# GpSimd's down-weight sums of a batch go behind its output tiles' scale operations, their halves and their store one batch later

## The reference

```
q, k, v = n(x) @ Wq, n(x) @ Wk, n(x) @ Wv            # n: layernorm over the 512 values
scores  = swap(q) @ swap(k).T / 4                     # 512 x 512 per batch: features attend to features
x       = x + n(swap(softmax(scores) @ swap(v)) @ Wo)
gate_w, up_w, down_w = spline(gate_cp), spline(up_cp), spline(down_cp)   # cubic, from few control points
x       = x + n((silu(n(x) @ gate_w.T) * (n(x) @ up_w.T)) @ down_w.T)    # inner width 2048
```

## Time and profile before

| | us |
|---|---|
| median of 3 runs (lowest to highest) | 900.88 (900.14 to 902.31) |
| the profiled execution | 904.34 |
| its span, first to last instruction | 902.5 |
| mean granted TensorE clock | 0.934 |

### The profile page before, as it was taken

How to read it: one execution, slowest core, us unless ns; L and a number is a source line. 1 busy time by engine, 2 the same in 40 slices (tenths; PEclk the granted TensorE clock), 3 DMA queues, 4 the chain that set the end, 5 groups by cost and what they waited for, 6 DMA issues and landing times. The chain is left out here.

```text
span 902.5 us, 19204 instructions
## 1 busy us (share of the span) xinstructions
PE 769.6 (85%) x7152; PEld 513.1 (57%) x7152; DVE 538.8 (60%) x1025; ACT 368.2 (41%) x632; POOL 440.3 (49%) x616
## 2 busy tenths in 40 slices
PE   5686999999999998984666988979879888897986
PEld 3564668776877685762232654636435555563455
DVE  6562753685377545654556667676667676863453
ACT  3321333232323232323445545555445555554541
POOL 4399459545944692032343444434444443543442
PEclk9797799999999998997796999999989999898999
DMA  8246147314741664058224063251622534315122
GB/s 304 105 156 193 66 152 266 122 46 163 245 131 35 196 214 99 2 189 285 84 87 148 6 202 123 91 191 49 198 85 86 188 103 154 128 59 200 48 72 72
DMA packets 64313, 120.54 MB, mean 134 GB/s; under 512 B 12144, under 2 KB 28656, under 8 KB 62192
## 3 DMA queue, kind: packets, MB, share of 16 engines
q1 hardware_dynamic: 64240, 119.53, 40.6%
HBM read 82.94 MB, written 36.57 MB: 132 GB/s over the span
## 5 line engine op out<-in xcount | busy, mean ns | idle before, releaser
L1194 POOL TENSOR_TENSOR act<-inter,act 128x512 f16<-128x512 f32 x128 | 152.5, 1194 | 87.6 <-ACT act L1234 87.4
L1304 DVE SCALAR_TENSOR_TENSOR inter<-ubank,c_up,gated 128x512 f32<-128x512 f32 x128 | 96.0, 750 | 99.3 <-ACT gated L1238 81.9
L1238 ACT ACTIVATE gated<-gbank,c_gate 128x512 f32<-128x512 f32 x128 | 88.0, 687 | 59.2 <-PE gbank L1401 58.9
L1441 PE MATMUL ybank<-down,act 128*128 128x160 f16 x512 | 110.7, 236 | 0.0
L1442 PE MATMUL ybank<-down,act 128*128 128x160 f16 x512 | 109.8, 235 | 0.0
L1443 PE MATMUL ybank<-down,act 128*128 128x160 f16 x512 | 109.7, 235 | 0.0
L1234 ACT CAST act<-inter 128x512 f16<-128x512 f32 x128 | 78.7, 615 | 43.8 <-DVE inter L1304 43.5
L1401 PE MATMUL gbank<-z,s_twice 128*32 128x512 f16 x512 | 53.7, 409 | 44.8 <-DMA z<-token_features 22.9
L897 POOL TENSOR_TENSOR hr<-hmv,heps 128x1 f32<-128x1 f32 x32 | 6.1, 192 | 162.4 <-DVE hmv L926 162.4
L1441 PEld LDWEIGHTS ybank<-down,act 128*128 128x128 f16 x512 | 50.4, 98 | 37.1 <-issue 36.6
L1401 PE MATMUL ubank<-z,s_twice 128*32 128x512 f16 x512 | 53.2, 406 | 19.9 <-DVE inter L1304 19.7
(11 more groups left out here) (190 smaller groups left out, 2178.0 us busy)
## 6 DMA issues: line engine op xcount, KB each, us to landing
x_ln<-x SPq DMA_DIRECT2D x64, 256.0 KB, 3.7
z<-token_features SPq DMA_DIRECT2D x16, 1024.0 KB, 6.6
job<-job_in SPq DMA_DIRECT2D x24, 640.0 KB, 5.4
shared<-x SPq DMA_DIRECT2D x32, 256.0 KB, 2.7
x<-shared SPq DMA_DIRECT2D x32, 256.0 KB, 2.0
token_features<-z_hi SPq DMA_DIRECT2D x64, 128.0 KB
token_features<-z_lo SPq DMA_DIRECT2D x64, 128.0 KB
x_res<-x SPq DMA_DIRECT2D x32, 256.0 KB, 2.7
```

The lines of the kernel that those rows point to most:

```text
L1194: pool.tensor_tensor(hidden[par][:, i, TOK:2 * TOK], inter[:, i % INTERS, :], hidden[par][:, i, 0:TOK], ALU.subtract).then_inc(inter_ready, 1)
L1238: act.activation(gated[:, slot % 2, :], gbank[:], ACT.Silu, scale=c_gate[:]).then_inc(silu_done, 1)
L1304: dve.scalar_tensor_tensor(out=inter[:, i % INTERS, :], in0=ubank[:], scalar=c_up[:], in1=gated[:, i % 2, :], op0=ALU.mult, op1=ALU.mult). ...
L1441: pe.matmul(out, hidden[par][:, r, high], box[:, 0], start=False, stop=False)
```

## The change

GpSimd, in batches 0 to 2: both unit weights first, then the next batch's `ln_scale` and the `y_scale`, then all six sums. In the last batch: unit weights, sums 0 and 1, unit weights, sums 2 to 5, and then the scales, as the sums have no batch behind them. In batches 1 to 3, ScalarE and VectorE take the halves of the batch before in the stages of the Gram matrix and of the first product; the last batch's own stay between its output tiles. SyncE stores a batch's halves behind `store_units` of the next, and issues job loads at the end of the body. The body of batch 0 is written out.

```diff
 SyncE
+            def store_jobs(b):
+                sp.wait_ge(job_ready, held(sp, (b + 2) * JOBS))
+                sp.dma_start(d_dram[held(sp, b)], job_out[:]).then_inc(d_stored, 16)
-            def body(b, more):
+            def body(b, first, more):
...
-                load_job(b, 2)
-                load_job(b, 3)
                 store_units(2 * b, True)
-                load_job(b, 4)
-                load_job(b, 5)
+                if not first:
+                    store_jobs(b - 1)
+                if not more:
+                    load_job(b, 2)
+                    load_job(b, 3)
                 store_units(2 * b + 1, more)
-                if more:
-                    load_job(b + 1, 0)
-                    load_job(b + 1, 1)
+                if not more:
+                    load_job(b, 4)
+                    load_job(b, 5)
...
                 if more:
                     load_res(b + 1, XR - 1)
-                sp.wait_ge(job_ready, held(sp, (b + 2) * JOBS))
-                sp.dma_start(d_dram[held(sp, b)], job_out[:]).then_inc(d_stored, 16)
+                    for k in range(2, JOBS):
+                        load_job(b, k)
+                    load_job(b + 1, 0)
+                    load_job(b + 1, 1)
+                else:
+                    store_jobs(b)
 GpSimd
             def body(b, more):
-                for c in range(2):
-                    sum_job(b, 2 * c)
-                    sum_job(b, 2 * c + 1)
-                    unit_weights(2 * b + c)
-                sum_job(b, 4)
-                sum_job(b, 5)
+                unit_weights(2 * b)
+                if not more:
+                    sum_job(b, 0)
+                    sum_job(b, 1)
+                unit_weights(2 * b + 1)
+                if not more:
+                    for k in range(2, JOBS):
+                        sum_job(b, k)
...
                     y_scale(b, t)
...
+                if more:
+                    for k in range(JOBS):
+                        sum_job(b, k)
 ScalarE (VectorE has the same with evac_lo, mirror_lo, job_lo)
-            def body(b, more):
+            def body(b, first, more):
                 for m in range(K):
                     evac_hi(b, 0, m, ga_hi, m * P, G_SCALE)
                     if m:
                         mirror_hi(b, m - 1)
+                        if not first:
+                            job_hi(b - 1, m - 1)
                 for m in range(K):
                     evac_hi(b, 1, m, tu_hi, 0, 1.0)
...
+                    if not first and m < K - 1:
+                        job_hi(b - 1, K - 1 + m)
...
-                    if 1 <= t <= JOBS:
+                    if not more and 1 <= t <= JOBS:
                         job_hi(b, t - 1)
 each of the four engines
-            with act.Fori(0, B - 1) as b:
-                body(b, True)
-            body(B - 1, False)
+            body(0, True, True)
+            with act.Fori(0, B - 2) as before:
+                body(before + 1, False, True)
+            body(B - 1, False, False)
```

More of the change, by code:

```diff
@@ L309, in _ @@
                 load_res(0, t)
-            with sp.Fori(0, B - 1) as b:
-                body(b, True)
-            body(B - 1, False)
+            body(0, True, True)
+            with sp.Fori(0, B - 2) as before:
+                body(before + 1, False, True)
+            body(B - 1, False, False)
             for q in range(XR):
@@ L567, in body @@
                         mirror_lo(b, m - 1)
+                        if not first:
+                            job_lo(b - 1, m - 1)
                 for m in range(K):
@@ L572, in body @@
                     dve.tensor_copy(xT_lo[:, m, :], tbank[:, 1, :].bitcast(F16)).then_inc(tb_lo, 1)
+                    if not first and m < K - 1:
+                        job_lo(b - 1, K - 1 + m)
                 if more:
@@ L632, in body @@
                                                  op0=ALU.subtract, op1=ALU.add).then_inc(x1_ready, 1)
-                    if 2 <= t < 2 + JOBS:
+                    if not more and 2 <= t < 2 + JOBS:
                         job_lo(b, t - 2)
@@ L683, in _ @@
             scales()
-            with dve.Fori(0, B - 1) as b:
-                body(b, True)
-            body(B - 1, False)
+            body(0, True, True)
+            with dve.Fori(0, B - 2) as before:
+                body(before + 1, False, True)
+            body(B - 1, False, False)
         @block.tensor
```

## The result

| | before | after |
|---|---|---|
| median (lowest to highest), us | 901.48 (900.14 to 902.31), 4 runs | 919.23 (917.79 to 926.13), 4 runs |
| profiled execution / its span, us | 904.34 / 902.5 | 926.13 / 924.3 |
| first matmul of batch 0's output tiles | 105.77 | 91.68 |
| first matmul of the FFN half | 421.37 | 439.91 |

The ratio of after to before is 1.0211, 95% interval 1.0164 to 1.0258. The forecast was 920.1 us, range 907 to 929. A ratio here compares the means of the fast runs, those at most 1.5% above the fastest of their kernel (for after with a fifth, of 919.39 us), while medians and ranges are of all runs, with one slow run each in the first and the third experiment (914.14 and 920.49 us).

What follows compares the result with a forecast made beforehand. The attention half is set by TensorE where GpSimd is early and by GpSimd where late; the FFN half is unchanged. Terms: -13.3 + 2 x 4.5 + 23.5 = +19.2 on median 900.88 gives 920.1 us, range 907 to 929.

Steps and rivals of the forecast that it cites:

- Batch 0: First batch: VectorE's 14.43 us wait for GpSimd's reciprocal deviation goes, fourth product falls from 24.16 to 10.88 us, -13.3 us.
- the bound at -20: Batch 0's largest gain, -20 us, if its third product gets batch 1's pace too.
- The load queue: Sums' loads behind the output tiles, no longer hidden: with 4.1 us loads, six sums take 22.4 us from S.
- S: Start of GpSimd's sums behind a batch's output tiles, from which the prediction counts its GpSimd times.
- Batches 1 and 2: Middle batches: reciprocal deviation 0.7 us late and second unit weights over the softmax normalisation; +4.5 us each, ends 0 and 6.7.
- Batch 3: Last batch: own six sums plus the previous batch's precede the first FFN scale, S + 59.8 for S + 36.3, +23.5 us.
- The halves: ScalarE's and VectorE's halves, moved into the next batch's first two products: taken at nothing; uncovered, each costs 0.8 us.
- (a): Rival: load gap covers the softmax, batch 0 gains 20.0 us, batches 1 and 2 gain 1.2 each; 896.9 us, faster; chance 0.05.
- (b): Rival: last batch's order is felt, middle batches free, batch 0 gains more; 901 to 908 us; chance 0.09 together with (e).
- (c): Rival: slow loads, each 640 KB one 5.1 us or more, and the lock in full; 930 us and up; chance 0.05.
- (d): Rival: batch 0's unit weights end after about 78, VectorE still stalls; 9 us gain left, +23; counted within forecast's 0.81.
- (e): Rival: halves were on the output tiles' path, 14.4 us back, 905.7 us; chance 0.09 together with (b).

Runs made afterwards that it cites:

- The first experiment: Changed kernel, but in the last batch GpSimd takes both unit weights, then the first FFN tiles' scales, its own six sums among and behind them: 905.3 us.
- the third experiment: Changed kernel with the second unit weights of batches 1 and 2 one column wide, their work left out: 914.7 us, ratio to before 1.0091.
- The thin sums: Kernel before the change with batch 0's six sums one column wide, loads and order kept: 893.29 us, ratio to before 0.9878.
- the fourth experiment: Changed kernel with all 48 half operations of ScalarE and VectorE one column wide: 919.52 us, ratio to before 1.0141.
- the last two experiments: Changed kernel with sums 0 and 1 between the unit weights, last batch's scales among its sums: 892.08 us; then also sums 2 and 3 between output-tile scales: 885.01 us.
- the last experiment: Kernel with sums 0 and 1 in the load gap, plus sums 2 and 3 of batches 0 to 2 cut between output-tile scales: 885.01 us, ratio to before 0.9808.

## Why the prediction was right

*Batch 0.* The forecast was that GpSimd's list ends at 72.5, VectorE is free at 73.6, and TensorE is next. Measured: 73.0, 73.1, and 10.88 us for the fourth product, the -13.3 us forecast. The further 6.7 us of the third product, the bound at -20, did not come, since the second unit weights still lie on that softmax. The thin sums show that those 6 us exist.

*The load queue.* S + 22.4 was forecast for the end of the sums, and 140.53 - 118.13 = 22.4 us was measured. Its parts hold too: load 2 was expected at S + 8.9 and sum 2 begins at S + 9.0; load 4 at 16.2 and sum 4 begins at 16.0; load 5 at 19.3 and sum 5 begins at 19.3. The load time chosen (4.1 us, against the median of 5.1 in before) decided this.

*Batches 1 and 2.* 4.5 us each was a choice between 0 and 6.7; it was 3.0 and 5.3, 8.3 together for 9.0. That the sum comes so near is in part luck, as the one was too high by 1.5 us and the other too low by 0.8. The mechanism is shown by the third experiment. The two parts were not equally right: the forecast's 0.7 us of VectorE waiting for a late reciprocal deviation never came, since the slowed softmax makes VectorE itself late, at S + 47.4 (165.56), past GpSimd's S + 46.1. The whole price was the softmax, and more than half of it reached TensorE as matmuls at the lower clock level (1.7 of 3.0 us and 3.1 of 5.3). It differs between two batches with the same code, and VectorE's own loss doesn't explain that: 3.0 and 3.2 us. The unit weights begin at 153.72 in one and at 245.11 in the other, 1.8 and 2.3 us behind the start of VectorE's L618 of the first block (151.95 and 242.82). In the first and the fourth experiment, where the code of these two batches' softmax is the same, this distance was 1.5 and 2.1, and 1.4 and 3.1 us, and the price 3.0 and 3.9, and 3.0 and 5.7 us, with VectorE's loss between 2.7 and 3.3 us each time. So the price rises with the distance, and the granted clock of the third product is 0.89 or 0.90 up to 3.9 us and 0.81 at 5.3 and 5.7. No run moved the distance alone, so that it is the cause is not shown.

By the Trainium skill ("SBUF — State Buffer", Who interferes with whom) VectorE was to lose 5.0 us a batch, an estimate; it lost 2.97 and 3.20 us. The 4.2 us that TensorE lost in the mean are another quantity, with the lower clock in it. The rule speaks of exclusion for a whole instruction, and the two rows at 154.15 and 155.60, longer by 0.93 and 1.18 us, lie within one instruction of the unit weights (0.4 to 1.6 us each), which agrees with it. L618 reads two tiles in SBUF; L615 reads one, and no run here shows whether it ran in a 2-port mode. Nor does one tell exclusion from a shared rate.

*Batch 3.* S + 59.8 was forecast, S + 59.2 measured; 23.5 us of loss forecast, 22.9 measured, and 1.1 us more behind it in the third product. The first experiment shows the loss to be the length of GpSimd's list ahead of the scale: 14.8 us less of list gave 14.9 us back, and the last two experiments continue the row (scale at S + 38.6 and S + 31.7, VectorE's wait 9.50 and 3.05 us).

*The halves.* Nothing forecast, nothing found in the fourth experiment.

*Rivals.* (a) wanted the load gap on the whole softmax; it covered one block of four in batch 1 (the gap ends at 153.72, the second block's normalisation begins at 154.15). Its further 1.2 us for each of batches 1 and 2 weren't there to gain either: with all eight operations of batch 1 undisturbed, in the third experiment, the third product takes 12.69 us, as in before, where two of them were longer. (b) wanted the middle batches free and 17 us from batch 0; they cost 3.0 and 5.3 us, and batch 0 gave 13.0. (c) needed slow loads; they landed in 3.9 us in the median. (d) would leave batch 0 a wait; none is there. (e) wanted 14.4 us back in the output tiles; the stage went from 24.02 to 23.76 us in batch 0 and from 23.99 to 23.92 in batch 1. The prediction's wording in (a) has 4.95 us as the time of four operations; the row counts eight.

## What to carry to other kernels

An engine off the critical path is a list with due times: write down when each consumer needs its item and what the list, load gaps included, can deliver by then. Moving work behind the hurried item helps only where a later stretch of the list has that much slack; here the first batch was 14 us late, the middle ones had 7.5 us of slack, and the last was 7 us late already, so what left the first came due there. Work is better put where the engine waits anyway: two sums in a load gap of 5 us and eight pieces of at most 0.9 us between scales, with the last batch's scales ahead of its last sums, turned a loss of 2.1% into a gain of 1.9%. And a load that nothing covers belongs in the list too: some 5 us behind a batch's first unit weights and 3.3 to 3.5 us among six sums here.

## What the runs showed of the hardware

A VectorE instruction took up to 2.9 times its time beside GpSimd's unit weights (in batch 1 of after L615: 0.49 and 1.42 us; L618: 0.75 and 1.93 us), and it works both ways: in the same batch of after GpSimd's addition L370 took 1.28 us ahead of the softmax and 1.61 us over it, L374 0.74 and 1.05 us. Where the two alternate instead, as in the first seven of the last experiment's output tiles, neither shows it (L676: 0.75 us; GpSimd's pieces: 0.53 to 0.88 us).

Such a delay costs TensorE more than VectorE's lost time. VectorE lost 3.20 us in batch 2 of after, TensorE 5.3 us: behind a wait of 2.40 and one of 1.05 us its matmuls took 0.79 and then 0.63 us each in place of 0.39, and the granted clock of the third product fell from 1.00 to 0.81.

The granted clock of the FFN half differs between executions with the same code there: 0.92 in the 440 us from its start in before and 0.90 in after, with TensorE busy for 367.90 and 371.13 us of them. The profiled executions' remaining 3 us lie in that half; what sets its clock stays open.
